# Two-layer preln kernel: low operand parts one slot behind the high parts, two score banks, two alternating projection banks

## The reference, cut to what matters

```python
h = _rms(x, ln_w)
q = (h @ wq).reshape(B, S, NHEADS, HEAD_DIM)
k = (h @ wk).reshape(B, S, KVHEADS, HEAD_DIM)
v = (h @ wv).reshape(B, S, KVHEADS, HEAD_DIM)
q, k = _rope(q, k)
...
scores = jnp.einsum('bqhd,bkhd->bhqk', q, k) / np.float32(np.sqrt(HEAD_DIM))
scores = jnp.where(causal[None, None], scores, jnp.float32(-1e+30))
attn = jax.nn.softmax(scores, -1)
o = jnp.einsum('bhqk,bkhd->bqhd', attn, v).reshape(B, S, NHEADS * HEAD_DIM)
x = x + o @ wo
```

## Time and profile before

| | |
|---|---|
| median of 3 runs | 2133.78 us (2124.33 to 2141.91) |
| the profiled execution's own time | 2130.15 us |
| its span in the trace | 2128.3 us |
| mean granted TensorE clock | 0.941 of full |
| busy over the span | PE 85%, DVE 59%, ACT 52%, POOL 42% |
| the 64-wide attention's scores (line 1776) | 1024 matmuls, 320.1 us busy |
| the low parts (line 1052, 128x256 form and one more) | 256 instructions, 102.6 us busy, 119.4 us idle before them |

### The profile page before, as it was taken

How to read it: one execution, slowest core, us unless ns; L and a number is a source line. 1 busy time by engine, 2 the same in 40 slices (tenths; PEclk the granted TensorE clock), 3 DMA queues, 4 the chain that set the end, 5 groups by cost and what they waited for, 6 DMA issues and landing times.

```text
span 2128.3 us, 36840 instructions
## 1 busy us (share of the span) xinstructions
PE 1799.8 (85%) x10666; PEld 1208.9 (57%) x10666; DVE 1248.9 (59%) x4282; ACT 1100.4 (52%) x2758; POOL 899.3 (42%) x1013
## 2 busy tenths in 40 slices
PE   4989899868787745999999999999999994799994
PEld 2656678733333323666666666666666663555552
DVE  5674454446686745666766666766666766622222
ACT  3324243235565423666666667666666672244442
POOL 3991000111221002545554445554445552588884
PEclk9989899958999987999999999999999996899997
DMA  5000020000001010000000000000000005455557
GB/s 150 1 1 1 1 60 1 0 0 1 1 1 40 0 43 1 1 1 1 1 1 1 1 1 0 0 1 1 1 1 1 1 0 199 140 83 84 82 83 165
DMA packets 61420, 61.34 MB, mean 29 GB/s; under 512 B 13136, under 2 KB 58320, under 8 KB 61264
## 3 DMA queue, kind: packets, MB, share of 16 engines
q0 software_dynamic: 15360, 20.98, 6.3%
q1 hardware_dynamic: 45904, 38.65, 5.6%
HBM read 40.48 MB, written 19.14 MB: 28 GB/s over the span
## 4 chain that ended last, share of the span: by engine, by line
PE 45%; issue 18%; DVE 17%; ACT 13%; POOL 3%; DMA 1%; DVEq 1%; SPq 0%; ACTq 0%; POOLq 0%
PE banks L1807 4%; PE banks L1995 3%; ACT wide_x L1440 3%; PE banks L1817 3%; PE banks L1871 3%; PE banks L1621 3%; PE banks L1846 2%; PE banks L1798 2%; PE banks L1776 2%; POOL wdT L724 2%; DVE wide_x L1052 2%; PE banks L1683 2%; ACT wugT L1454 2%; ACT wdT L1406 2%; PE banks L1913 2%
## 5 line engine op out<-in xcount | busy, mean ns | idle before, releaser
L1776 PE MATMUL banks<-wide_k,wide_q 128*128 128x512 f32 (+3 forms) x1024 | 320.1, 395 | 0.5 <-ACT wide_k L1398 0.5
L656 POOL TENSOR_TENSOR wugT<-wugT,con 128x512 f32<-128x512 f32 (+1 forms) x256 | 236.2, 934 | 119.2 <-DVE con L1015 119.2
L1406 ACT ACTIVATE wugT<-wugT,con 128x512 f32<-128x512 f32 (+1 forms) x256 | 170.5, 666 | 98.6 <-DVE con L1033 96.3
L1817 PE MATMUL banks<-late,xnT 128*128 (+1 forms) x512 | 196.5, 507 | 20.1 <-DVE xn L1046 16.4
L1776 PEld LDWEIGHTS banks<-wide_k,wide_q 128*128 128x128 f32 x1024 | 172.9, 191 | 52.5 <-issue 13.6
L1062 DVE TENSOR_REDUCE con<-banks 128x2 f32<-128x1024 f32 x128 | 154.6, 1213 | 67.6 <-PE banks L1859 66.6
L667 POOL TENSOR_TENSOR attn<-attn 128x320 f32<-128x320 f32 x128 | 111.2, 869 | 159.9 <-DVE attn L1003 159.3
L1052 DVE TENSOR_TENSOR wide_x<-attn,wide_x 128x256 fp32r<-128x256 f32 (+1 forms) x256 | 102.6, 441 | 119.4 <-ACT wide_x L1440 119.4
L1798 PE MATMUL banks<-attn 128*64 128x256 f32 x1280 | 169.5, 390 | 3.6 <-DVE attn L1041 3.6
L1033 DVE CUSTOM_DVE_ANT_0 wugT<-banks,wide_mask 128x512 f32<-128x512 f32 (+1 forms) x256 | 157.9, 617 | 6.9 <-issue 6.9
L1995 PE MATMUL banks<-w,late 128*128 x320 | 156.3, 611 | 2.4 <-issue 1.5
(11 more groups left out here) (312 smaller groups left out, 4211.8 us busy)
## 6 DMA issues: line engine op xcount, KB each, us to landing
w<-in_L_ffn_w_dram SPq DMA_DIRECT2D x32, 256.0 KB, 6.1
late<-in_L_ffn_w_dram SPq DMA_DIRECT2D x16, 256.0 KB, 6.2
y_rows<-wqkv1T SPq DMA_DIRECT2D x1, 2176.0 KB, 7.9
x<-in_L_attn_x_dram SPq DMA_DIRECT2D x4, 512.0 KB, 9.1
late<-in_L_ffn_wq_dram SPq DMA_DIRECT2D x2, 1024.0 KB, 7.5
late<-in_L_ffn_wo_dram SPq DMA_DIRECT2D x1, 2048.0 KB, 8.1
h_rows<-wugT SPq DMA_DIRECT2D x1, 2048.0 KB, 7.0
y_rows<-x SPq DMA_DIRECT2D x1, 2048.0 KB, 13.2
```

The costliest lines, as they stand in the source:

```text
L656: nc.gpsimd.tensor_tensor(p, p, rinv[:, m:m + 1].to_broadcast([P, n]), ALU.mult).then_inc(at.sem["norm"], 1)
L1406: nc.scalar.activation(at.prob(m)[:, 0:n], at.prob(m)[:, 0:n], ACT.Exp, bias=negmax[:, m:m + 1], scale=-1.0, accum_out=rowsum[:, m:m + 1]) ...
L1776: ins = nc.tensor.matmul(sbank[:, 0:keys], wide_q[:, side, i, qcols], wide_k[:, side, w, 0:keys], start=(w == 0), stop=(w == 1))
L1817: ins = nc.tensor.matmul(bank[YBANK][:, 0:QKV], xnT[:, c, P * wide_tile(a):P * wide_tile(a) + P], w_qkv(n, c), start=(c == 0), stop=(c == ...
```

## The change

Four things change, all in the 64-wide attention. The entry `split` becomes two: `high` (ScalarE) stays where `split` was, and `low` (VectorE) moves into the next slot, at its head: behind that slot's max and reciprocal. The scores get two banks in place of three, so the scores of every unit a now wait for the max of unit a-2. The bank set free (bank 2) becomes a second bank for `qkv` and `project`, which alternate between banks 7 and 2, and in the steady loop each waits only until the use before the last has been emptied (`n_y - spare`). The prologue and the first, last and drain windows keep waiting for all of them.

```diff
--- before.py
+++ after.py
@@ -337,11 +337,12 @@
-                return SBANK[1 if unit == self.units - 1 else unit % 3]
-
-            def units_in_use(self, unit):
-
-                return 1 if unit in (1, self.units - 1) else 2
+                return SBANK[unit % 2]
+
+            def ybank(self, kind, a):
+
+                order = [(k, e) for k, _d, e in self.windows["steady"] if k in ("qkv", "project")]
+                return bank[YBANK[(order.index((kind, a)) + 1) % 2]]
@@ -373,17 +374,17 @@
                 3: [("turn", -1, 9)],
-                4: [("project", -1, 2), ("split", 1, 0)],
-                5: [("values", -1, 9), ("qkv", 1, 1)],
+                4: [("project", -1, 2), ("high", 1, 0)],
+                5: [("low", 1, 0), ("values", -1, 9), ("qkv", 1, 1)],
                 6: [("turn_qk", 1, 0)],
-                7: [("project", -1, 3), ("turn_qk", 1, 1), ("turn", 0, 0), ("split", 1, 1)],
-                8: [("turn", 0, 1), ("qkv", 1, 2)],
+                7: [("project", -1, 3), ("turn_qk", 1, 1), ("turn", 0, 0), ("high", 1, 1)],
+                8: [("low", 1, 1), ("turn", 0, 1), ("qkv", 1, 2)],
                 9: [("turn_qk", 1, 2), ("turn", 0, 2)],
-                10: [("turn_qk", 1, 3), ("turn", 0, 3), ("split", 1, 2), ("qkv", 1, 3)],
-                11: [("turn", 0, 4)],
+                10: [("turn_qk", 1, 3), ("turn", 0, 3), ("high", 1, 2), ("qkv", 1, 3)],
+                11: [("low", 1, 2), ("turn", 0, 4)],
                 12: [("turn_qk", 1, 4), ("turn", 0, 5), ("values", 0, 0), ("values", 0, 1), ("values", 0, 2), ("values", 0, 3),
-                     ("split", 1, 3)],
-                13: [("turn_qk", 1, 5), ("turn", 0, 6)],
+                     ("high", 1, 3)],
+                13: [("low", 1, 3), ("turn_qk", 1, 5), ("turn", 0, 6)],
                 14: [("turn_qk", 1, 6), ("project", 0, 0)],
@@ -398,7 +399,7 @@
                 if t >= 1:
-                    ops.append(("split", 0, t - 1))
+                    ops += [("high", 0, t - 1), ("low", 0, t - 1)]
                     ops += [("turn_qk", 0, pieces * (t - 1) + i) for i in range(pieces)]
@@ -411,7 +412,7 @@
         a2 = Attention("a2", [(r, 0) for r in reversed(range(TB))], HD64, True, wide_bufs, 10, 2, 2, WIDE)
-        SBANK, PTBANK, OBANK, MBANK, YBANK = (0, 1, 2), (3, 4), 5, 6, 7
+        SBANK, PTBANK, OBANK, MBANK, YBANK = (0, 1), (3, 4), 5, 6, (7, 2)
         N_OBANK, N_MBANK = 6, 7
@@ -993,7 +994,7 @@
                 hd, h = at.hd, t % 2
-                src = bank[YBANK][:, 0:320].rearrange("p (h d) -> p h d", d=hd)
+                src = at.ybank("qkv", t)[:, 0:320].rearrange("p (h d) -> p h d", d=hd)
                 first_of = lambda name: mid(name)[0] + wide_tile(t) * hd
@@ -1002,7 +1003,7 @@
                                         ALU.mult).then_inc(at.sem["rope"], 1)
-                vp = bank[YBANK][:, 320:384]
+                vp = at.ybank("qkv", t)[:, 320:384]
                 if reached(n - 1):
@@ -1043,10 +1044,10 @@
                         rows = res[:, bass.ds(b(n) * TB + r, 1), :]
-                        nc.vector.tensor_tensor(rows, rows, bank[YBANK][:, None, 0:D], ALU.add).then_inc(at.sem["yb"], 1)
+                        nc.vector.tensor_tensor(rows, rows, at.ybank("project", a)[:, None, 0:D], ALU.add).then_inc(at.sem["yb"], 1)
                     elif kind == "qkv":
                         rope(at, n, a, wide_v[:, (par + d) % 2, wide_tile(a), :])
-                    elif kind == "split":
+                    elif kind == "low":
                         v.wait_ge(at.sem["hi"], n * TB + a + 1)
@@ -1434,7 +1435,7 @@
                         nc.scalar.activation(xnT[:], all_xT[:, :, bass.ds(b(n) * S, S)], ACT.Copy).then_inc(at.sem["stage"], 1)
-                    elif kind == "split":
+                    elif kind == "high":
                         act.wait_ge(at.sem["sum"], n * TB + a + 1)
@@ -1759,6 +1760,7 @@
+                spare = 1 if ops is at.windows["steady"] else 0
                 for kind, d, a in ops:
@@ -1770,8 +1772,8 @@
                             pe.wait_ge(at.sem["m_sb"], n * at.turns + at.turns)
-                        if reached(n * at.units + a - at.units_in_use(a)):
-                            pe.wait_ge(at.sem["max"], n * at.units + a - at.units_in_use(a))
+                        if reached(n * at.units + a - 1):
+                            pe.wait_ge(at.sem["max"], n * at.units + a - 1)
                         for w in range(2):
@@ -1800,11 +1802,11 @@
                         pe.wait_ge(at.sem["o_sb"], n * TB + a + 1)
-                        pe.wait_ge(at.sem["yb"], n_y)
+                        pe.wait_ge(at.sem["yb"], n_y - spare)
                         ring = at.onT.shape[1]
...
                         for c in range(chunks):
-                            ins = nc.tensor.matmul(bank[YBANK][:, 0:D], at.onT[:, a % ring, P * c:P * c + P], w_out(n, c),
+                            ins = nc.tensor.matmul(at.ybank("project", a)[:, 0:D], at.onT[:, a % ring, P * c:P * c + P], w_out(n, c),
                                                    start=(c == 0), stop=(c == chunks - 1))
@@ -1812,9 +1814,9 @@
                         if reached(n_y):
-                            pe.wait_ge(at.sem["yb"], n_y)
+                            pe.wait_ge(at.sem["yb"], n_y - spare)
                         for c in range(DC):
-                            ins = nc.tensor.matmul(bank[YBANK][:, 0:QKV], xnT[:, c, P * wide_tile(a):P * wide_tile(a) + P], w_qkv(n, c),
+                            ins = nc.tensor.matmul(at.ybank("qkv", a)[:, 0:QKV], xnT[:, c, P * wide_tile(a):P * wide_tile(a) + P], w_qkv(n, c),
                                                    start=(c == 0), stop=(c == DC - 1))
...
```

## The result

| | before | after |
|---|---|---|
| median of 4 runs on one chip | 2137.85 us | 2215.71 us (2209.21 to 2220.72) |
| the profiled execution's time, its span | 2130.15, 2128.3 | 2217.82, 2215.9 |
| mean granted TensorE clock | 0.941 | 0.932 |

The ratio is 1.037, 95% interval 1.031 to 1.043: the change makes the kernel 78 us slower. The forecast was 2188 in a range of 2121 to 2208: the sign is right, the size is not. The sum was made against the profiled execution. It had 58 us of loss, and 87.7 were measured.

What follows compares the result with a forecast made beforehand. The prediction took TensorE, busy 806 of 870 us, and its waits as the bound. It summed 2130.15 + 67.3 (moved low parts) - 9.0 (second projection bank) = 2188 us, range 2121 to 2208.

Steps and rivals of the forecast that it cites:

- The bank: Second projection bank removes qkv's residual-add wait behind each jump, a score-bank max wait replaces it: 9.0 us gained on 15 passes.
- Low 0: Tile 0's subtraction also waits for a third normalising: done 1311.36, not 1310.50; rope 0.35 us late, won back by TensorE.
- Low 1: Tile 1's subtraction meets unit 6's normalising: transposes at 1316.40 instead of 1315.92, tile 3's qkv about 0.44 us late.
- Low 2: Tile 2's subtraction falls behind tile 3's rope and a max, meeting rope add and normalising: TensorE's transposes 2.0 us late.
- Low 3: Tile 3's subtraction meets unit 11's normalising: transposes at 1327.46 instead of 1325.29, making 2.17 us per round in all.
- the 67.3: Total loss from the moved low parts in the 64-wide attention: 31 rounds of 2.17 us, 67.3 us.
- signs to look for: Trace values expected in the 64-wide attention if right, such as two rounds taking 62 us in place of 58.33.
- Slower still: Rival: TensorE's longer waits drop its clock to 1.2 GHz for a tenth of the loop, some 40 us more, 2230; chance 0.10.
- no collision: Rival: GpSimd starts later, each low part takes 0.63 us, transposes of tile 2 0.3 late; 2124 us; chance 0.17.
- Faster: Rival: the freed VectorE brings TensorE to tile 3's qkv 0.6 us earlier each round; 28 us gained, 2102; chance 0.09.

Runs made afterwards that it cites:

- banks_only: Changed kernel with the low parts back in their old places, keeping two score banks and two projection banks; ratio 0.9927 to the kernel before.
- after_thin_warm: Changed kernel with GpSimd normalising only one column per unit, 20 unused TensorE transposes before the wait for low part 2, and one wait moved; ratio 0.9976 to before.
- after_warm: Changed kernel with 20 unused TensorE transposes before its wait for low part 2, and one wait for ScalarE's copy moved ahead of them; ratio 1.0200 to before.
- after_thin_norm: Changed kernel with GpSimd's normalising cut to one column of each unit, all orders and waits kept; ratio 1.0083 to the kernel before, median 2162.2 us.
- low_moves_only: Kernel before with only the four low parts moved, keeping three score banks and one projection bank; ratio 1.0495 to the kernel before.
- low01_back: Changed kernel with low parts 0 and 1 back in their old slots, 2 and 3 still moved; ratio 1.0258 to the kernel before.
- before_thin_norm: Kernel before with GpSimd's normalising cut to one column of each unit; ratio 0.9988 to the unedited kernel before.

## Why the prediction was right about the collisions and wrong in its number

The kernels with one and with both parts removed split the loss. Beside each term stands its size by the ratios (of 2137.85 us) and by the profiled spans:

| part | from, to | by ratios | by spans | predicted |
|---|---|---|---|---|
| second projection bank, two score banks | before, banks_only | -15.6 | -10.8 | -9.0 |
| later places of the low parts | banks_only, after_thin_warm | +10.5 | +13.1 | } +67.3 |
| collisions with the normalising | after_thin_warm, after_warm | +47.9 | +55.5 | } |
| TensorE's clock behind its wait, with some 6.5 of the moved wait | after_warm, changed | +36.8 | +29.8 | 0 |
| all | | +79.5 | +87.6 | +58.3 |

The rows aren't clean cuts. `after_thin_warm` still has the rope add at low 2, has lost the collision that low 0 had before, and carries the transposes and the moved wait. In the other order, normalising first and clock second, the collisions take 62 us by ratios and 54.5 by spans, and the clock 23 and 31.

The periods of undisturbed rounds hold no clock and no added work. From `banks_only` to the changed kernel they give 62.19 - 57.45 = 4.74 us per two rounds, 2.37 a round where 2.17 was predicted, 73.5 us in 15.5 pairs of rounds; from the kernel before to `banks_only` 0.88, 13.6 us. The difference is 59.9 us, against 58.3 predicted.

**The bank**: right in place and near in size. The wait for the max came, at the place the prediction gave, 0.7 us long in the mean.

**Low 0**: predicted to set TensorE's transposes 0.36 late (1311.42 against 1311.06); by the starts behind rope 0's, they are 0.42 late. **Low 1**: 0.48 predicted, 0.45 measured; the qkv of tile 3 0.44 and 0.48. In its detail the step for low 1 was wrong: the first subtraction got in 0.14 us ahead of the normalising (1233.89 against 1234.03) and the second alone had to wait. **Low 2**, "the dear one": 2.01 late predicted, 2.15 measured; rope, max, rope add, subtraction, normalising, subtraction stand in the predicted order. **Low 3**: 2.17 and 2.34. 

So the 67.3 is met by 73.5 in periods, and by 68.6 in spans and 58.4 in ratios, which are low by the moved wait. Of the signs to look for, the period of two rounds (62 against 62.19), VectorE's wait (under 30, was 5.7), TensorE's wait for the low parts (110 predicted, 102.6 in 870 to 1740 and 106.7 in 910 us), the qkv wait and the one for the max all came. The mean of the 128x256 subtraction did not: 721 ns, not 850; the 128x128 one, put at over 500, has 773. Who waits for a whole instruction is more often the second subtraction.

**What failed is the clock**, which the sum took to stay full: it put nothing for it, and the runs show 20 us in the 29 rounds between the markers and about 23 in the whole span (29.8 less the 6.5 of the moved wait). By the ratios, less the moved wait, it lies between 21 and 30. The prediction had the mechanism as a rival, "Slower still": TensorE idle for over 4 us a round with one wait of 2 us, clock at the lower level for part of the loop, 40 us. In undisturbed rounds TensorE is idle 31.68 - 27.87 = 3.8 and 30.5 - 26.0 = 4.5 us, with a wait of 2.10, so the condition was met. The mistake was to set it beside the main case as an alternative with a chance of 0.10, when the main case's own result, a wait of 2 us in every round, is its condition. With 23 beside the 67.3 and the 9.0 the sum comes to 2212, and with the measured 73.5 and 13.6 to 2213; the profiled execution took 2217.82. The last 4 to 5 us are not placed.

The **no collision** rival is met by `after_thin_warm`, which has none with the normalising: 2124 was given for it, 0.997 of 2130.15, and it measured 0.998. Its reasoning, that the order alone eats what the free VectorE gives, holds in size. Taken from the start of rope 0, in an undisturbed round of `after_thin_norm`, TensorE comes to the qkv of tile 3 0.77 us earlier than in rows 6 (0.6 was given), and to the transposes of tile 2 0.47 later (0.3). **Faster** never had a footing: `low_moves_only` shows 1.05.

The Trainium skill, page "SBUF — State Buffer", section "Who interferes with whom", was cited for the exclusive lock. The trace agrees for whole instructions: each of the three second subtractions ends 0.15 us behind a GpSimd instruction. By the page alone the sum lay between 2161 and 2188, and the rows after decide for the upper end: at lows 0, 1 and 2 a GpSimd instruction goes between two subtractions that follow each other at once. The Trainium skill, page "TensorE: Matmul & The Clock Gate", section "HAM oscillation — how this bites in real kernels", was cited for a kernel that gained nothing further by double-buffering PSUM. A second bank does gain here: `banks_only` has 0.9927, all of its interval below 1.

**What stays open**: why the clock falls in 13 rounds and not in the other 16. They have the same waits, but do not fall evenly: 10 of the 15 rounds of the shorter kind (30.5 us) are slow and 3 of the 14 of the longer kind. Neither the length of the wait nor the short waits before it decide it: 1.69 us without them gives 14 slow rounds, 2.11 us without them gives 4.

## What to carry to other kernels

When a change makes TensorE wait longer in every round, price its clock in the same sum, as a consequence and not as a rival. An instruction with two SBUF inputs on VectorE should not stand directly behind the one that releases GpSimd; ask what GpSimd is doing at that moment, and what is next in its queue. And an idle engine's wait (here 112 us of VectorE) is worth only the time at which its result comes: the cure was an earlier producer, not a later consumer.

## What the runs showed of the hardware

- Two subtractions in a row do not hold GpSimd off: it gets one whole instruction in between them (low 1: 0.96 us where it was 0.83; low 2: 0.80 where 0.61 is usual). The second subtraction then ends 0.15 us behind it. At low 3 there is only one in the way, and the pair ends 0.48 behind it. GpSimd pays a little too: its mean for 128x512 rose from 1040 to 1085 ns, for 128x256 from 613 to 666.
- TensorE's granted clock fell behind waits of 2.10 us in 13 rounds of 29 (changed), behind waits of 1.69 us in 14 of 29 (`after_thin_norm`), behind waits of 2.11 us in 4 of 29 (`low01_back`), and in none with 20 transposes in the wait (`after_warm`, `after_thin_warm`). Over four microseconds at the end of such a wait and behind it, it was 0.57 and 0.61, where it is 1.00 before. The price was 20 us in the loop, some 23 of 2216 in all.
- It needs no wait of that length: `before_thin_norm` has one slow round, at a granted clock of 0.94, and the wait just ahead of it is of 1.24 us, for the residual add:

```profile
1272.61 2.05 PE L1817 MATMUL banks<-late,xnT 128*128 x4 [1.24 <-DVE xn L1046]
```
